# Context values of a decoder layer: split one-pass products in place of f32 products, and moved mask reductions

## What is computed

```python
x = x + self_attention(layernorm(x), Wq, bq, Wk, bk, Wv, bv, Wo, bo)      # 16 heads, causal

h = layernorm(x)                                                          # cross-attention
scores = einsum('bsd,bmd->bsm', h, ctx) / sqrt(256)                       # m: 512 context rows
scores = where(mask[:, None, :], scores, -1e30)
readout = einsum('bsm,bmd->bsd', softmax(scores), ctx)
x = x + where(any(mask, axis=-1)[:, None, None], readout, 0)

x = x + moe(layernorm(x))                                                 # 16 experts, top 4
```

## Time and profile before

| | us |
|---|---|
| median of 3 runs (lowest, highest) | 218.2 (217.79, 218.23) |
| the profiled execution, its own time | 219.71 |
| its span, first to last instruction | 218.0 |

### The profile page before, as it was taken

How to read it: one execution, slowest core, us unless ns; L and a number is a source line. 1 busy time by engine, 2 the same in 40 slices (tenths; PEclk the granted TensorE clock), 3 DMA queues, 4 the chain that set the end, 5 groups by cost and what they waited for, 6 DMA issues and landing times.

```text
span 218.0 us, 4415 instructions
## 1 busy us (share of the span) xinstructions
PE 210.3 (96%) x1392; PEld 175.3 (80%) x1392; DVE 163.0 (75%) x448; ACT 131.0 (60%) x248; POOL 93.5 (43%) x83
## 2 busy tenths in 40 slices
PE   7799999899999899999999999999999999999995
PEld 2687766676688699899899898898898898898893
DVE  3579698969669667988898786785785786786754
ACT  3437899747642814567866775765665675666340
POOL 7689997018201120067436624614615516516000
PEclk9789999999999999999999999999999999999999
DMA  6994430000000000013442243042152141210002
GB/s 185 314 397 159 146 103 0 0 5 2 3 0 0 0 5 0 0 38 111 144 117 58 117 144 110 35 144 91 53 144 67 77 144 46 98 48 0 0 0 98
DMA packets 8062, 17.45 MB, mean 80 GB/s; under 512 B 960, under 2 KB 3184, under 8 KB 7920
## 3 DMA queue, kind: packets, MB, share of 16 engines
q1 hardware_dynamic: 7616, 16.97, 23.8%
q10 hardware_dynamic: 432, 0.31, 0.5%
HBM read 16.75 MB, written 0.52 MB: 79 GB/s over the span
## 4 chain that ended last, share of the span: by engine, by line
PE 84%; DVE 8%; ACT 2%; DMA 2%; issue 1%; POOL 1%; SPq 0%; DVEq 0%; ACTq 0%
PE PS L1305 35%; PE PS L1321 20%; PE PS L1109 5%; PE PS L1179 3%; PE PS L1095 2%; DMA wqkv<-wqkv_d 2%; PE PS L1099 2%; PE PS L1157 2%; PE PS L1122 2%; PE PS L1146 2%; PE PS L1350 2%; PE PS L1272 1%; ACT pr L515 1%; PE PS L1129 1%; PE PS L1165 1%
## 5 line engine op out<-in xcount | busy, mean ns | idle before, releaser
L343 POOL TENSOR_TENSOR WLg<-raw_g,WHg 128x1024 fp32r<-128x1024 f32 x16 | 38.4, 2403 | 68.6 <-ACT WHg L475 68.5
L1305 PE MATMUL PS<-XH,WHg 128*128 128x512 f32 x120 | 47.0, 391 | 0.0
L1305 PE MATMUL PS<-XL,WHg 128*128 128x512 f32 x120 | 46.9, 391 | 0.0
L1305 PE MATMUL PS<-XH,WLg 128*128 128x512 f32 x120 | 46.7, 389 | 0.0
L945 DVE TENSOR_SCALAR pt<-pt 128x512 f32<-128x512 f32 x30 | 24.8, 826 | 20.6 <-ACT pt L608 20.6
L1321 PE MATMUL PS<-WHd,HH 128*128 128x256 f32 x120 | 34.0, 283 | 0.2 <-DVE HL L954 0.2
L1321 PE MATMUL PS<-WLd,HH 128*128 128x256 f32 x120 | 34.0, 283 | 0.0
L1321 PE MATMUL PS<-WHd,HL 128*128 128x256 f32 x120 | 34.0, 283 | 0.0
L614 ACT ACTIVATE HH<-pt 128x512 fp32r<-128x512 f32 x30 | 18.9, 630 | 17.9 <-DVE pt L949 17.9
L608 ACT ACTIVATE pt<-PS,bup 128x512 f32<-128x512 f32 x30 | 20.6, 687 | 13.5 <-PE PS L1305 13.5
L515 ACT ACTIVATE pr<-masked,nmax 128x128 f32<-128x128 f32 x64 | 23.8, 445 | 8.2 <-DVE nmax L819 8.0
(11 more groups left out here) (196 smaller groups left out, 373.6 us busy)
## 6 DMA issues: line engine op xcount, KB each, us to landing
raw_g<-we_d SPq DMA_DIRECT2D x16, 512.0 KB, 4.1
raw_w<-we_d SPq DMA_DIRECT2D x16, 256.0 KB, 2.7
ctxT<-ctxT_d SPq DMA_DIRECT2D x1, 1024.0 KB, 9.9
ctx_sb<-ctx_d SPq DMA_DIRECT2D x1, 1024.0 KB, 12.2
wqkv<-wqkv_d SPq DMA_DIRECT2D x3, 256.0 KB, 5.0
out_d<-x SPq DMA_DIRECT2D x4, 128.0 KB, 1.8
rows<-rows_d SPq DMA_DIRECT2D x1, 264.0 KB, 6.6
x<-x_d ACTq DMA_DIRECT2D x2, 128.0 KB, 3.2
```

The lines of the kernel that those rows point to most:

```text
L343: g.tensor_tensor(WLg[slot][:, :, :, :].rearrange("p k g f -> p (k g f)"), raw_g[slot][:, :], WHg[slot][:, :, :, :].rearrange("p k g f -> ...
L1305: i = t.matmul(PS[:, 2 * m + part, :], w[slot][:, k, part, m * P:(m + 1) * P], xx[:, k, :], start=(n == 0), stop=(n == 3 * KD - 1))
```

## The change

It has four parts.
1. The context rows are split. POOL makes `ctx_high` and `ctx_low` (`split_context`, two instructions for each batch), that of batch 0 ahead of `rstds(1)` and that of batch 1 behind it. `ctx_low` takes the place of `ctx_sb` in memory.
2. The turned probabilities are split. ACT's copy is now the high part `xpt_high`; a new DVE step `context_low(c)` makes `xpt_low`, PSUM minus high part, 128x512. The bank of chunk 1's turn is 0 instead of 4.
3. PE has 12 one-pass products for each chunk in place of 4 f32 products: eight in `context_values_high`, which need ACT's part alone, and four in `context_values_low`, which wait for DVE's.
4. The order moves. On PE, `context_values_low(1)` stands between the high and the low scores of chunk 2. On DVE, `context_weight(0)`, `context_out(0)` and `context_stats(0)` stand further back, and `context_low(1)` stands between the low parts of chunks 2 and 3. The two `valid` reductions are at steps 7 and 8 of the head loop instead of 10 and 12.

```diff
-        xpt = [keys_flat[:, (2 + i) * M:(3 + i) * M].rearrange("p (c q) -> p c q", q=P) for i in range(2)]
...
-        XS_BANK, XT_BANK, XV_BANK = (3, 2, 4, 5), (3, 4, 6, 3), (1, 2, 4, 5)
+        XS_BANK, XT_BANK, XV_BANK = (3, 2, 4, 5), (3, 0, 6, 3), (1, 2, 4, 5)
...
             masks()
+            def split_context(b):
+
+                pool.wait_ge(ctx_in, 16)
+                chunks = slice(b * KM, (b + 1) * KM)
+                g.tensor_copy(ctx_high[:, chunks, :], ctx_sb[:, chunks, :]).then_inc(ctx_high_done, 1)
+                pool.wait_ge(ctx_high_done, b + 1)
+                g.tensor_tensor(ctx_low[:, chunks, :], ctx_sb[:, chunks, :], ctx_high[:, chunks, :].bitcast(F32), ALU.subtract
+                                ).then_inc(ctx_low_done, 1)
+
+            split_context(0)
             rstds(1)
+            split_context(1)
...
-                a.activation(xpt[c % 2].rearrange("p h q -> p (h q)"), PS[:, XT_BANK[c], :], ACT.Copy
+                a.activation(xpt_high[:, c % 2].rearrange("p h q -> p (h q)"), PS[:, XT_BANK[c], :], ACT.Copy
...
+            def context_low(c):
+
+                dve.wait_ge(xpt_done, c + 1)
+                if c >= 2:
+                    dve.wait_ge(xav_done, c - 1)
+                v_.tensor_tensor(xpt_low[:, c % 2].rearrange("p h q -> p (h q)"), PS[:, XT_BANK[c], :],
+                                 xpt_high[:, c % 2].rearrange("p h q -> p (h q)").bitcast(F32), ALU.subtract).then_inc(xlow_done, 1)
...
-                if v in (10, 12):
-                    b = (v - 10) // 2
+                if v in (7, 8):
+                    b = v - 7
...
-            context_weight(0)
+            context_low(0)
             residual(1, 0, PS[:, 6, 0:D])
             residual(1, 1, PS[:, 5, 0:D])
             centre(1)
+            context_weight(0)
+            low_tokens(7, yh_done, 2, slice(S, S + P), yl_done)
+            context_low(1)
+            low_tokens(3, yh_done, 3, slice(S + P, T), yl_done)
+            context_scale(1)
             context_out(0)
             context_stats(0)
-            low_tokens(7, yh_done, 2, slice(S, S + P), yl_done)
-            low_tokens(3, yh_done, 3, slice(S + P, T), yl_done)
-            context_scale(1)
             context_weight(1)
...
             normalise(x3, 4, (0, 1))
+            context_low(2)
             context_weight(2)
             context_weight(3)
+            context_low(3)
...
-            def context_values(c, blocks=range(KM)):
+            def context_values_high(c, blocks=range(KM)):
                 pe.wait_ge(xpt_done, c + 1)
+                pe.wait_ge(ctx_low_done, c // QC + 1)
                 for j in blocks:
...
+                    for n, w in enumerate((ctx_high, ctx_low)):
+                        t.matmul(PS[:, XV_BANK[c], 0:D], xpt_high[:, c % 2, j, :], w[:, (c // QC) * KM + j, :],
+                                 start=(j == 0 and n == 0), stop=False)
+
+            def context_values_low(c):
+                pe.wait_ge(xlow_done, c + 1)
+                for j in range(KM):
+                    i = t.matmul(PS[:, XV_BANK[c], 0:D], xpt_low[:, c % 2, j, :], ctx_high[:, (c // QC) * KM + j, :],
+                                 start=False, stop=(j == KM - 1))
+                i.then_inc(xav_done, 1)
...
-            context_values(0, range(0, KM // 2))
+            context_values_high(0, range(0, KM - 1))
...
             context_turn(1)
-            context_values(0, range(KM // 2, KM))
-            context_values(1, range(0, KM // 2))
+            context_values_high(0, range(KM - 1, KM))
+            context_values_low(0)
+            context_values_high(1)
             for j in range(QC):
                 pe.wait_ge(xn_done, NC + QC + j + 1)
                 turn_chunk(xn, QC + j, (7, 3)[j])
-            context_values(1, range(KM // 2, KM))
-            for c in (2, 3):
-                context_scores_high(c)
-                context_scores_low(c)
+            context_scores_high(2)
+            context_values_low(1)
+            context_scores_low(2)
+            context_scores_high(3)
+            context_scores_low(3)
             context_turn(2)
             transposes(xn, 0, 0, xn_done, NC + 3 * QC)
             context_turn(3)
-            context_values(2)
-            context_values(3)
+            context_values_high(2)
+            context_values_low(2)
+            context_values_high(3)
+            context_values_low(3)
             logits_of(1, (0, 1))
```

More of the change, by code:

```diff
@@ L65, in decoder_layer @@
         rest_of_wqkv = sb("rest_of_wqkv", [P, KD, D])
-        ctx_sb = sb("ctx_sb", [P, B * KM, D])
+        raw_ctx = ExitStack()
+        ctx_sb = raw_ctx.enter_context(nc.sbuf_tensor("ctx_sb", [P, B * KM, D], F32))
+        raw_ctx.close()
+        ctx_low = sb("ctx_low", [P, B * KM, D], F32R)
+        ctx_high = sb("ctx_high", [P, B * KM, D], F32R)
         wo = sb("wo", [P, KD, D])
@@ L97, in decoder_layer @@
         wqkv_high, wqkv_low = (sb(n, [P, 3, KD, D], F32R) for n in ("wqkv_high", "wqkv_low"))
-        kT = sb("kT", [P, KD, T])
+        self_keys = ExitStack()
+        kT = self_keys.enter_context(nc.sbuf_tensor("kT", [P, KD, T], F32))
+        self_keys.close()
+        xpt_low = sb("xpt_low", [P, 2, KM, P], F32R)
         qpar = sb("qpar", [P, KD, 2, T])
@@ L103, in decoder_layer @@
         pt = sb("pt", [P, 2, HG, BLK, P])
-        masked = sb("masked", [P, 2, 2, BLK * P])
+        self_scores = ExitStack()
+        masked = self_scores.enter_context(nc.sbuf_tensor("masked", [P, 2, 2, BLK * P], F32))
+        self_scores.close()
+        xpt_high = sb("xpt_high", [P, 2, KM, P], F32R)
+        rest_of_masked = sb("rest_of_masked", [P, P * KM])
         nmax = sb("nmax", [P, 2, 2, QC])
@@ L208, in decoder_layer @@
         out_done = sem("out_done")
+        xlow_done, ctx_high_done, ctx_low_done = sem("xlow_done"), sem("ctx_high_done"), sem("ctx_low_done")
         dbias_zero, dbias_split, score3_zero, score_parts = (sem(n) for n in ("dbias_zero", "dbias_split", "score3_zero", "score_parts"))
-        XS_BANK, XT_BANK, XV_BANK = (3, 2, 4, 5), (3, 4, 6, 3), (1, 2, 4, 5)
+        XS_BANK, XT_BANK, XV_BANK = (3, 2, 4, 5), (3, 0, 6, 3), (1, 2, 4, 5)
         NV = 2 * B * NG
@@ L1240, in _ @@
             turn_chunk(att, 2, 7)
-            pe.wait_ge(ctx_in, 16)
-            context_values(0, range(0, KM // 2))
+            context_values_high(0, range(0, KM - 1))
             pe.wait_ge(att_done, NC)
```

## The result

| | median us (lowest, highest) | executions |
|---|---|---|
| before | 217.99 (217.73, 220.36) | 20 |
| after | 219.03 (217.94, 219.92) | 20 |

The ratio after to before is 1.0035, with a 95% interval of 1.0018 to 1.0052: slightly slower. The forecast was 218.7 us. The executions of after don't scatter around their median, they lie at two levels. Nine are at 217.94 to 218.37 us with a mean granted clock of 0.999 or 1.00; eleven are at 219.03 to 219.92 with 0.992. The median, 219.03, lies at the lower edge of the second level. The number cannot be understood without the two, so both are told from here on.

What follows compares the result with a forecast made beforehand. The prediction took PE to bound the kernel, with DVE late in places. Full-speed terms summed to -0.4 us; with the clock falling, the middle was +0.5 us on 218.2, giving 218.7 us, range 217.4 to 219.2.

Steps and rivals of the forecast that it cites:

- a clock that falls behind a new gap: PE's clock falls behind the idle gap ahead of `context_turn(2)`: 218.7 us (218.4 to 219.1), chance 0.45.
- the sum at full speed: All terms to the last turn of `xn` chunk 2, with PE's clock held: 0.4 us less than before.
- Masks: Moving the `valid` reductions to steps 7 and 8 of the head loop gains 1.08 us by 51.31 us.
- case 4: Reduction at step 7 is held by POOL's subtraction; held 2.2 us, it gives 219.4 us; chance 0.05.
- "Cost 0" of the split on POOL: POOL's two added casts (1.05 us) and subtractions (2.37 us) delay nothing that is waited for: cost 0.
- PE's 0.31 us ahead of the turn of `xn`: One-pass products take 1.4 us off PE, 0.31 us of it ahead of the turn of `xn` chunk 2.
- DVE to `context_max(2)`: From the low part of chunk 2 to `context_max(2)`, DVE takes 3.6 us instead of 2.12; start at 70.0.
- PE's gap: PE idles 2.15 us ahead of `context_turn(2)`, against 0.61 before.
- The last turn: The last turn of `xn` chunk 2 comes at 79.3 us against 79.71.
- The clock: Behind PE's gap the clock falls in most executions, for about 3.4 us: +0.7 or +0.3 us, middle +0.5.
- Case 2: The clock holds and DVE bounds from 66 to 79 us: 217.8 us (217.5 to 218.2), chance 0.43.
- Cases 3: DVE's additions fit into waits for ScalarE, `context_max(2)` starts before 69.4, PE bounds: 217.4 us, chance 0.07.

Runs made afterwards that it cites:

- before, undisturbed: Second trace of before, nothing changed, clock at 1.00 from 8.8 to 12.2 us; that run of before measured 217.94 us, ratio 1.0002.
- experiment 5: After, run once more unchanged: 218.80 us, ratio 1.0045 to before.
- experiment 3: After with POOL's `split_context(1)` moved ahead of `rstds(1)`: 217.90 us, ratio 1.0008 to before.
- experiments 6: After with `context_out(0)` and `context_stats(0)` back ahead of the two low parts of the tokens: 217.38 us, ratio 0.9980 to before.
- 7: After with `split_context(1)` ahead of `rstds(1)`, and `context_out(0)` and `context_stats(0)` back ahead of the tokens' low parts: 216.96 us, ratio 0.9959 to before.
- 9: After with `split_context(1)`, `context_out(0)` and `context_stats(0)` placed earlier, and `context_weight(2)` ahead of `context_low(2)`: 216.70 us, ratio 0.9945 to before.
- 2: Before with only the two `valid` reductions moved to steps 7 and 8: 216.73 us, ratio 0.9945 to before.
- 10: After with chunks 0 and 1 back to f32 products, only batch 1's rows split, ahead of `rstds(1)`, `context_weight(2)` ahead of `context_low(2)`: 216.07 us, ratio 0.9916 to before.
- 11: Before with only the two `valid` reductions moved, run once more: 216.69 us, ratio 0.9949 to before.

## Why the prediction was right, and where it was not

The forecast, 218.7 us by a clock that falls behind a new gap, is close to the medians of 219.03 and 218.80, and the mechanism is the one that ran. As a sum it was too low: 0.4 us less than before at full speed and 0.5 more with the fall, so 0.9 for the fall itself. Measured, the two levels are 0.2 more (218.16 against 217.99) and 1.3 more (219.30). The price of the fall was nearly right; the sum at full speed was 0.6 off. The forecast was made for executions in which the clock falls, and their level, 219.30, lies above even the upper end of the stated range, 219.2. That the median comes within 0.3 us is luck in part: the fall took place in eleven executions of twenty, and with two fewer the median would have been that of the upper level, near 218.3.

- **Masks**: 1.08 us predicted, 1.1 to 1.2 measured in the time, and 1.12 in the traces, which is the 1.30 at every step from `context_max(0)` on less the shift of 0.18. Right. The DVE step behind the second reduction (`x`, line 751 or 773) is at 46.42 in before, undisturbed, and at 45.10 in after.
- **The reduction beside POOL** (case 4): both took 0.68 us. The first, which case 4 had beside the subtraction, ran beside POOL's cast instead (31.64, the cast from 31.13 to 32.18); the second, at 33.88, lay within the subtraction of 32.26 to 34.65. The rule of the Trainium skill on `tensor_reduce` (SBUF — State Buffer, section "Who interferes with whom": on trn2 it never contends with GpSimd), which no row of before tested, has its row now, and the trace agrees:

```profile
33.88 0.68 DVE L877 TENSOR_REDUCE valid<-mask 128x1 f32<-128x512 uint8 x1
```

```profile
32.26 2.39 POOL L398 TENSOR_TENSOR keys_low<-ctxT,keys_high 128x1024 fp32r<-128x1024 f32 x1
```

- **"Cost 0" of the split on POOL**: this term of the sum failed. It followed who waits for POOL's results, and found nobody. It did not ask what DVE runs beside POOL. Price 0.46 us in the trace; its removal gave 0.42 to 0.44.
- **PE's 0.31 us ahead of the turn of `xn`**: of it 0.07 arrived. From `context_max(0)` to that turn it is 9.99 us in after, 10.06 with the masks alone. The last eight products there took 1.20 us, 0.15 each instead of 0.119: the first of them started at 63.41, right behind ACT's copy of chunk 1 (62.76 to 63.36). In this place PE was bound by the copy and not by its own rate, and a faster product ahead of it only waits longer:

```profile
62.76 0.60 ACT L551 ACTIVATE xpt_high<-PS 128x512 fp32r<-128x512 f32 x1 [0.99 <-PE PS L1207]
```

- **DVE to `context_max(2)`**: 3.6 us predicted, 3.56 measured; 2.12 before. The largest term of the sum, and right. That all gains were gone there was right too. By the prediction it starts at 68.3 us on the scale of after's trace (70.0 less 1.56 and less the shift of 0.18); it was 68.94, later by the two terms above, 0.46 and 0.24.
- **PE's gap**: 2.15 us predicted, 1.81 measured. The two terms above move both ends of the gap and don't explain this. From the turn of `xn` to the end of the scores PE took 4.59 us (64.47 to 69.06); the prediction had 4.05 (65.7 to 69.75; by its own terms, 71.22 less 1.39, it should have been 69.83). The two f32 products that had followed that turn covered PE's wait for ScalarE; with them gone PE idles 0.25 us ahead of the scores of chunk 2, and the four low products of chunk 1, put between the scores, take 0.58 us (66.45 to 67.03). `context_turn(2)` came 6.40 us behind the turn of `xn` (predicted 6.2), which is why only 0.34 of the 0.54 us is missing from the gap.
- **The last turn**: by the prediction 79.3 against 79.71, 0.4 us early. Here the working mixed two views. 79.71 is the chain's time, in which a queued PE instruction begins when the one ahead of it ends; by the timeline of that same trace the turn started 0.16 us sooner:

```profile
79.55 0.38 PE L1014 MATMUL PS<-ident,xn 128*128 128x128 f32 x2
```

  A wait for DVE ends at a real start, and so must be set against the timeline's. The sum should have been -0.25, not -0.41. With the lock (+0.46), PE's 0.24 that didn't arrive, and the masks' 1.12 in place of 1.08 (-0.04), it is +0.4. The traces show 0.17 (78.16 against 77.99), or 0.35 with the shift of 0.18; the times of the upper level show 0.17 in the first comparison (218.16 against 217.99) and 0.32 in experiment 5 (218.22 against 217.90).
- **The clock**: "in most executions" was 15 of 28 for this kernel, 19 of 40 with experiment 3. The price, 0.9 by the prediction (0.7 to 1.1, the clock falling in place of holding), was 1.0 to 1.1 us. It came out at the upper end because the fall began at 70.7, right behind the gap, and not at the values: the first value product was 2.26 us behind `context_turn(2)` instead of 1.74 (70.27 to 72.53, 70.87 to 72.61), so the turns were not hidden as the lower end had it. The Trainium skill, TensorE: Matmul & The Clock Gate, section "Why this matters for your kernels", warns only of longer gaps than this one, and the prediction took it that by this rule the clock would hold; here it did not in 19 of 40 executions, and the measurement decides.

Case 2 (the clock holds) describes the executions of the upper level, but for those 0.6 us. Cases 3 (DVE not late) and 4 (the reduction held by POOL) did not come about; what case 4 describes happened to another operation, `xscale`.

What stays open is why the same kernel, with the same gap, has its clock fall in one execution and not in the next.

## What to carry to other kernels

A cheaper form of a product pays only where the engine it runs on is what is waited for, and the halves of one change can differ in that: here the split gained 0.6 us for two chunks (216.07 against 216.69) and lost as much for the other two in the best order tried (216.70 with all four), and only a version with one half showed it. Before an operation is added to GpSimd, look not only at who needs its result but at which VectorE operations run beside it. And set ends of one engine against starts in the timeline, not in the chain. Before two traces are compared, look at a step ahead of the change: here such a step was up to 0.4 us apart between traces (`keys_high` at 30.87 to 31.28 us in the changed kernels and 31.31 in before, undisturbed).

## What the runs showed of the hardware

- A GpSimd subtraction of 128x1024 with both inputs in SBUF held a VectorE `TENSOR_SCALAR` of 128x2 until it ended, 1.37 us instead of 0.16; one of 128x256 was held for 2.1 us; a GpSimd cast of 128x1024 held one of 128x2 for 0.47 us. A VectorE subtraction and a copy that read PSUM (0.69 and 0.55 us) and the mask reduction (0.68 us) took their usual times beside such a subtraction.
- With PE idle for 1.8 us between stretches of nearly full work, the mean granted clock was 0.992 in 19 of 40 executions; in the one of them that was traced, the clock was at 1.2 GHz for 3.4 us behind the gap. With gaps of 1.03 us (experiments 6, 7 and 9) this happened in none of 20 executions, with 0.6 us in none of 15 (2, 10 and 11). Each fall cost 1.0 to 1.1 us.
- The early fall in before (8.7 to 12.1 us) was in its first trace, two executions of the first twenty had a like time (220.3 us), and none of the 67 later ones that are counted had a mean clock under 0.999, with the same code. A single trace was therefore off by 1.6 us in all its later times.
